# Moving two weight transposes, eight adds, a compare, some bank copies and the row turns inside a decoder kernel

## The reference

```
x = LN(x + attention(x))             # 16 heads of 8, rotary positions, causal
x = LN(x + cross(x, ctx, mask))      # 16 heads of 8, with biases
x = LN(x + experts(x))               # 8 experts of 512, the best 2 per token
x = LN(x + attention(x))             # "wide": 16 heads of 64, not causal
x = LN(x + cross(x, ctx, mask))      # 16 heads of 8
x = LN(x + proj(LN(gelu(fc(x)))))    # weights rounded to -1, 0, 1
```

## Time and profile before

| | |
|---|---|
| three executions | 369.69, 370.45, 370.66 us (median 370.45) |
| profiled execution, its own time | 367.09 us |
| its span | 365.1 us |
| granted TensorE clock, mean | 0.970 |
| TensorE / VectorE / ScalarE / GpSimd busy | 88% / 63% / 50% / 52% |
| stream `pre` and its drain | to about 120 us |
| routed experts | about 120 to 195 us |
| stream `post` | about 200 us to the end |

### The profile page before, as it was taken

How to read it: one execution, slowest core, us unless ns; L and a number is a source line. 1 busy time by engine, 2 the same in 40 slices (tenths; PEclk the granted TensorE clock), 3 DMA queues, 4 the chain that set the end, 5 groups by cost and what they waited for, 6 DMA issues and landing times.

```text
span 365.1 us, 10567 instructions
## 1 busy us (share of the span) xinstructions
PE 321.6 (88%) x4062; PEld 265.6 (73%) x4062; DVE 230.6 (63%) x537; ACT 180.8 (50%) x395; POOL 191.6 (52%) x281
## 2 busy tenths in 40 slices
PE   3878998998798599999996897899999988899993
PEld 2546776877697499999995864676778556787763
DVE  1459986788846434573336477845666466787685
ACT  2247776787547533323314243544354443888641
POOL 2526998575677545543305756312222145487685
PEclk9999999899959999999999699999999999999999
DMA  6799998000011211111101110000000000000001
GB/s 190 230 319 266 292 300 246 4 2 4 15 45 38 73 31 46 50 54 45 32 27 36 45 31 16 0 4 0 2 2 2 3 3 2 2 4 2 4 22 36
DMA packets 35978, 23.02 MB, mean 63 GB/s; under 512 B 4160, under 2 KB 33882, under 8 KB 35802
## 3 DMA queue, kind: packets, MB, share of 16 engines
q1 hardware_dynamic: 34618, 19.64, 18.4%
q0 software_dynamic: 1024, 2.10, 2.0%
q10 hardware_dynamic: 288, 0.62, 0.5%
HBM read 14.60 MB, written 7.73 MB: 61 GB/s over the span
## 4 chain that ended last, share of the span: by engine, by line
PE 64%; DVE 14%; issue 8%; POOL 6%; ACT 4%; DMA 3%; SPq 1%; POOLq 0%; ACTq 0%; DVEq 0%
PE banks L933 7%; PE banks L923 7%; PE banks L1741 6%; PE banks L1710 6%; PE banks L1718 6%; PE banks L461 5%; PE banks L634 5%; PE banks L968 3%; PE banks L607 2%; PE banks L560 2%; PE banks L1125 2%; DVE mx L426 2%; PE banks L1483 2%; PE banks L947 2%; PE banks L586 1%
## 5 line engine op out<-in xcount | busy, mean ns | idle before, releaser
L470 ACT ACTIVATE PT<-banks 128x512 f32<-128x512 f32 x64 | 35.0, 598 | 24.3 <-PE banks L461 23.8
L974 ACT ACTIVATE U<-banks 128x512 f32<-128x512 f32 x40 | 23.9, 597 | 36.7 <-PE banks L933 21.3
L1698 POOL COPY U<-WALL 128x1024 f32 x23 | 23.8, 1040 | 32.2 <-PE banks L1718 29.4
L334 POOL TENSOR_SCALAR ve<-mv 128x1 f32<-128x1 f32 x40 | 9.4, 234 | 56.3 <-DVE mv L329 55.7
L1733 DVE TENSOR_TENSOR PT<-banks,PR 128x512 f32<-128x512 f32 x23 | 15.9, 691 | 34.5 <-PE banks L1718 30.3
L449 ACT ACTIVATE PR<-PR 128x1024 f32<-128x1024 f32 x32 | 33.8, 1057 | 7.0 <-DVE PR L443 7.0
L461 PE MATMUL banks<-cst,PR 128*128 128x128 f32 x256 | 34.8, 280 | 0.5 <-DVE rk L1577 0.4
L923 PE MATMUL banks<-XT,WQKV 128*128 128x128 f32 x256 | 33.2, 292 | 0.4 <-ACT XT L1905 0.4
L923 PEld LDWEIGHTS banks<-XT,WQKV 128*128 128x128 f32 x256 | 31.7, 205 | 1.1 <-ACT XT L1905 0.7
L426 DVE TENSOR_REDUCE mx<-banks 128x16 f32<-128x1024 f32 x24 | 29.3, 1219 | 4.7 <-PE banks L618 3.2
L933 PE MATMUL banks<-WALL,XT 128*64 128x512 f32 x128 | 29.8, 601 | 2.8 <-DVE U L974 2.8
(11 more groups left out here) (192 smaller groups left out, 720.6 us busy)
## 6 DMA issues: line engine op xcount, KB each, us to landing
routed_rows<-zero SPq DMA_DIRECT2D x1, 4544.0 KB, 19.5
WALL<-in_L_ffn_wg_dram SPq DMA_DIRECT2D x8, 256.0 KB, 5.5
WALL<-in_L_ffn_wu_dram SPq DMA_DIRECT2D x8, 256.0 KB, 5.8
WALL<-in_L_ffn_wd_dram SPq DMA_DIRECT2D x8, 256.0 KB, 6.4
U<-in_L_attn_W_qkv_dram SPq DMA_DIRECT2D x1, 1536.0 KB, 6.9
XG<-routed_rows SPq DMA_DIRECT2D x23, 64.0 KB, 1.8
routed_rows<-YS SPq DMA_DIRECT2D x23, 64.0 KB, 1.6
cst<-shape_constants ACTq DMA_DIRECT2D x1, 537.0 KB, 4.4
```

What stands on the lines that cost most here:

```text
L470: act.activation(PT[:, n % 2, 4 * m:4 * m + 4, :].rearrange("p r q -> p (r q)"), PS[:, B_PT + m, :], ACT.Copy).then_inc(self.pt.sem, 1)
L974: return eng.activation(o, s, ACT.Copy) if part == 0 else eng.tensor_copy(o, s)
```

## The change

Weight groups 2 and 3 leave `later` and become `weights`, with one bank, number 4. Group 2 is turned in step 4 and copied by ScalarE, group 3 in step 5 and copied by VectorE; TensorE waits for bank 4 to be read before each, and for the copy behind each. The residual adds of `a0` move from steps 3 to 10 (one each) to steps 1 to 4 (two each). The bias adds that follow `a0` move from steps 6 to 13 to steps 10 to 17. The compare for `mrb` moves from VectorE, step 4, to GpSimd, step 5. ScalarE copies all wide fills below 20. A wide tile's row is turned in front of the q projection instead of behind the transposes of exponentials, its copy stands ahead of ScalarE's q copy, and the waits are changed to match; where the last wide tile meets the first narrow one, the narrow tile's transposes come before the wide tile's weighted values.

```diff
-        later = Transposes("later", [x_group(1), c_group(0), c_group(1), ([], [(gw[:, :], 8)], gwT[:, :]), w_group(1), w_group(2)], [6, 7])
+        later = Transposes("later", [x_group(1), c_group(0), c_group(1), ([], [(gw[:, :], 8)], gwT[:, :])], [6, 7])
+        weights = Transposes("weights", [w_group(1), w_group(2)], [4])
...
             def x_pe(self, pe, job):
                 pe.wait_ge(*self.norm.ln.at(i + 1))
                 if self.wide:
-                    if i + 1 < NT:
-                        pe.wait_ge(*self.norm.r.at(i + 2))
-                    beside = job.ahead(5)
+                    last = job.ahead(4)
+                    if last.stage.narrow:
+                        pe.wait_ge(*last.stage.q_read(last.i))
+                        pe.wait_ge(*last.stage.k_read(last.i))
...
             def x_act(self, act, job):
-                o, k = job.after, job.ahead(5) if self.wide else job.ahead(6)
-                if o and o.stage.narrow and not self.wide:
+                o, b = job.after, job.ahead(5)
+                if self.wide and b.stage.narrow:
+                    act.wait_ge(*(b.stage.k_mm if b.k_first() else b.stage.q_mm).at(b.i + 1))
+                elif o and o.stage.narrow and not self.wide:
                     act.wait_ge(*o.r_read())
...
             def by(self, f):
-                return DVE_FILLS[self.kind(f)]
+                return DVE_FILLS[self.kind(f)] if f >= 20 else 0
...
             # va_pe of wide tiles
                 if job.before:
                     pe.wait_ge(*job.before.r_read())
-                if job.ago(2):
-                    pe.wait_ge(*job.ago(2).x_read())
+                    pe.wait_ge(*job.before.x_read())
...
             # stream_pe
+                for x in turned(tiles, j):
+                    if x.stage.wide:
+                        x.stage.x_pe(pe, x)
                 if b:
                     b.stage.q_pe(pe, b)
...
-                if v and v.stage.wide:
+                last_wide = v and v.stage.wide and t and not t.stage.wide
+                if v and v.stage.wide and not last_wide:
                     v.stage.va_pe(pe, v)
                 if t:
                     t.stage.t_pe(pe, t)
+                if last_wide:
+                    v.stage.va_pe(pe, v)
...
             # stream_act
+                for x in turned(tiles, j):
+                    if x.stage.wide:
+                        x.stage.x_act(act, x)
                 if b:
                     b.stage.q_act(act, b)
...
         def pre_pe(pe, j, part):
             if j in (1, 2) and part == 2:
-                later.pe(pe, ((0, 1), (2, 3, 4, 5))[j - 1])
+                later.pe(pe, ((0, 1), (2, 3))[j - 1])
...
+            if j in (4, 5) and part == 0:
+                for s in pre[j - 3].v_read():
+                    pe.wait_ge(*s)
+                if j == 5:
+                    pe.wait_ge(*pre[0].y_read())
+                weights.pe(pe, (j - 4,))
+            if j in (4, 5) and part == 1:
+                weights.done(pe, j - 3)
...
             # pre_act
+            if j == 4 and part == 1:
+                weights.copies(act, 0, (0,))
...
             # pre_dve
+            if j == 5 and part == 0:
+                weights.copies(dve, 1, (1,))
...
-            if j == 4 and part == 1:
-                dve.tensor_scalar(mrb[0:6, :, :], mri[0:6, :, :], 0.0, None, ALU.is_equal).then_inc(s_mk, 1)
...
         def pre_pool(pool, j, part):
-            pass
+            if j in (1, 2, 3, 4) and part == 2:
+                for i in (2 * j - 2, 2 * j - 1):
+                    a0.res_pool(pool, pre[i])
+            if j == 5 and part == 2:
+                pool.wait_ge(s_m, 16 * 4)
+                pool.tensor_scalar(mrb[0:6, :, :], mri[0:6, :, :], 0.0, None, ALU.is_equal).then_inc(s_mk, 1)
+            if j >= 10 and part == 2 and j - 10 < NT:
+                a0.bias_pool(pool, pre[j - 10])
...
             # sync
+            weights.done(sp)
             later.done(sp)
```

More of the change, by code:

```diff
@@ L355, in decoder_kernel @@
             y_dve = ya_dve = sum_dve = max_dve = sub_dve = qk_dve = none
-            mask_pool = blocks_pool = cos_pool = res_pool = hidden_pool = bias_pool = shares_pool = none
+            mask_pool = blocks_pool = cos_pool = hidden_pool = bias_pool = shares_pool = none
             wide = early = narrow = False
@@ L375, in x_pe @@
                     beside = job.ahead(6)
-                if beside and beside.stage.narrow:
-                    for s in beside.first_read():
-                        pe.wait_ge(*s)
+                    if beside and beside.stage.narrow:
+                        for s in beside.first_read():
+                            pe.wait_ge(*s)
                 if self is a1 and i == 2:
@@ L1309, in stream_pe @@
                     t.stage.t_pe(pe, t)
+                if last_wide:
+                    v.stage.va_pe(pe, v)
                 if v:
                     v.stage.vb_pe(pe, v)
-                for x in turned(tiles, j):
-                    x.stage.x_pe(pe, x)
                 if b and b.stage.narrow and not b.k_first():
                     b.stage.k_pe(pe, b)
+                for x in turned(tiles, j):
+                    if not x.stage.wide:
+                        x.stage.x_pe(pe, x)
                 if y:
@@ L1343, in stream_act @@
                 for x in turned(tiles, j):
-                    x.stage.x_act(act, x)
+                    if not x.stage.wide:
+                        x.stage.x_act(act, x)
                 if b and b.stage.narrow and not b.k_first():
@@ L1407, in stream_pool @@
                 for x in turned(tiles, j):
-                    x.stage.bias_pool(pool, x)
-                if t:
-                    t.stage.res_pool(pool, t)
+                    if tiles is post:
+                        x.stage.bias_pool(pool, x)
                 extra(pool, j, 2)
@@ L1934, in pre_act @@
             if j in (1, 2) and part == 2:
-                later.copies(act, 0, ((0, 1), (2, 3, 4, 5))[j - 1])
+                later.copies(act, 0, ((0, 1), (2, 3))[j - 1])
+            if j == 4 and part == 1:
+                weights.copies(act, 0, (0,))
             if j == len(pre) and part == 1:
@@ L1940, in pre_dve @@
             if j in (1, 2) and part == 2:
-                later.copies(dve, 1, ((0, 1), (2, 3, 4, 5))[j - 1])
+                later.copies(dve, 1, ((0, 1), (2, 3))[j - 1])
+            if j == 5 and part == 0:
+                weights.copies(dve, 1, (1,))
             if j == 3 and part == 1:
```

6 lines of the change are left out of this document (2 added, 4 removed).

## The result

The first measurement gave 357.69 us against 370.07, a ratio of 0.9739 (95% interval 0.9685 to 0.9793). The profiled execution took 356.69 (span 354.9), against 367.09 (365.1). The change was then measured again in two sittings, on two chips.

| | runs | lowest | median | mean | highest |
|---|---|---|---|---|---|
| before, all | 59 | 365.08 | 367.37 | 367.81 | 374.01 |
| changed, all | 16 | 356.53 | 361.24 | 361.05 | 366.79 |
| before, kept | 54 | 365.08 | 367.27 | 367.42 | 370.66 |
| changed, kept | 11 | 356.53 | 359.03 | 359.46 | 363.37 |

What follows compares the result with a forecast made beforehand. TensorE, busy 88% of 365.1 us, was taken as the main bound, with VectorE and GpSimd full from 42 to 47. 2.8 + 2.4 + 0.85, called 6.1, off the median 370.45 gave 364.3, range 361.0 to 367.8.

Steps and rivals of the forecast that it cites:

- The level: Whole kernel: the gain was taken from the three runs' median 370.45, 3.4 above the profiled 367.09, giving 364.3.
- The sum: Whole kernel: 2.8 for the first stream, 2.4 for fills and 0.85 for turned rows, called 6.1 us.
- part 3: Second stream's wide fills on ScalarE: TensorE's stalls of 1.84 and 0.93 go, XT costs 0.69; 2.4 us gained.
- part 4: Second stream, steps 9 to 12: wide rows turned earlier end q projections' waits for XT; 0.85 us gained.
- part 2: First stream: residual adds moved off GpSimd's steps 6 to 8 and compare onto GpSimd; 0.4 us gained, once.
- The range: Whole kernel: 361.0 to 367.8 us at 8 in 10; under 1.1 us counted as no change.
- rival A: TensorE's instruction-stream pause near 63 and slow pace, 2.7 us: gone, 361.6 (chance 0.12); another, 367.0 (0.18, shared with B).
- part 1: First stream: weight groups 2 and 3 leave step 2; 4.1 us less 0.96 and 0.5 leaves 2.65.
- allowance: Step 3 of the first stream: TensorE mostly at fast pace; 0.2 us allowed, 0.9 if all slow.
- B: Steps 4 and 5: weight transposes cost 2.05 each, or a late input uses up 4.1; 367.0, shared chance 0.18.
- C: Step 10: mask rows landing after 61.2 delay tile 8's scores, making the kernel slower; chance 0.04 with its like.
- Theory P: From the held-back-load experiments: TensorE pauses without releaser come from instruction transfers among loads on the same DMA engines.

Runs made afterwards that it cites:

- e5: The changed kernel measured again without edit, beside the kernel before: 360.52 us against 367.39, ratio 0.9830.
- e12: The changed kernel with the narrow stages' x turned ahead of the k projection again: 362.11 us, ratio 0.9857 to the kernel before.
- e11: The changed kernel with residual adds, bias adds and compare back in their old places: 363.39 us, ratio 0.9874 to the kernel before.
- e8: The kernel before with only the wide fills below 20 moved to ScalarE: 364.69 us, ratio 0.9902 to the kernel before.
- e2: The kernel before with wide fills on ScalarE, turned rows and the new places of x and k: 364.75 us, ratio 0.9944 to the kernel before.
- e6: The changed kernel with loads of W_qkv and experts 4 to 7 held back until step 10's scores: 361.85 us, ratio 0.9781 to the kernel before.
- e9: The changed kernel measured a third time, on the chip of the last three experiments: 362.48 us against 367.23, too wide for a ratio.
- e7: The kernel before with loads of W_qkv and experts 4 to 7 held back until step 10's scores: 366.29 us, ratio 0.9979.
- e10: The changed kernel with only wide tile 7's row turned late, behind step 12's k projection: 361.73 us, ratio 0.9834 to the kernel before.

## Why the prediction missed

**The level, the step that failed.** The sum of 6.1 stands between the runs' differences (6.1 to 8.2) at their lower end. But "there is time in them that I cannot see; I take the same difference from the median" carried it from 367.09 to 370.45. That median of three was high: of the 56 other runs of the kernel before only seven reach 369.69, the lowest of those three, and the median of all 59 is 367.37, next to the profiled execution's 367.09. From there the sum gives 361.3, against 361.24 over all runs of the changed kernel and 359.03 over those kept. The first measurement's 357.69 is the same thing on the other side: three of its four runs are among the four fastest of sixteen, and the fourth is the slowest. So of the 6.6 us between forecast and measurement 3.1 are the level and 3.5 lie between 357.69 and the median of all sixteen. By that share, seven of 56, three runs of the kernel before would all lie so high once in some 500 times if each were drawn by itself; what held them together, when the fourth of that sitting took 365.42, is open.

**The sum, right in part by luck.** It left out the swap of x and k, which gave 0.5 to 1.0 from s4 to s10 and 0.13 behind, and put part 3 0.4 too low; part 4 gave 0.5 to 0.6 less than forecast and part 2 0.1 to 0.4 less. Together the stretches give about 6.4: 2.1 up to s4, 1.1 to s10 (28.08 to 26.97, the mean of five), 0.1 to s15, 2.8 for the fills and 0.3 for the rows.

**The range, the second failure.** I knew one pause of 1.20 and one slow stretch, made rival A of them, and gave it 2.7 us and 0.12; and I took 1.1 us for what can't be told from no change, where single runs of the kernel before scatter with a standard deviation of 1.9. The runs show such things in many places. Step 3 ran at full pace in two of the nine executions that had part 1 and cost about 1 us more in the rest; the pauses from s4 to s10 take 0.17 (e5) to 3.29 (e12) together; s15 to W0 moves by 3.3 us. Its first part, up to the first gathered tile, in windows of e5 and e11:

```profile
82.97:116.34 33.37, 24.57 (x290) 21.30 (x286) 24.04 (x109) 20.11 (x47) 22.40 (x29) 0.95 0.11 37
```
```profile
85.00:122.58 37.58, 29.99 (x289) 26.58 (x286) 23.87 (x109) 20.32 (x47) 21.77 (x28) 0.77 0.10 32
```

But for one bias add on GpSimd these are the same instructions, with a granted clock of 0.95 in 33.37 us and of 0.77 in 37.58. The changed kernel's runs span 10 us. A range of 6.8 around one number had no room for them.

**Part 1, right.** Scores of tile 1 at 19.1 forecast, 19.21 to 19.45 in nine executions. In the first profile step 4 lost 1.03 (5.31 for 4.28) where I had 0.96, step 5 0.33 (5.52 for 5.19) where I had 0.5. The 0.80 in step 5, though it names no releaser, stands in all nine executions: it is the wait for VectorE's copy that I had walked, not a pause like the others. Up to s4 the nine average 34.71, against 36.82 for the five without part 1: 2.1, where 2.65 less an allowance of 0.2 was forecast. The term that was mis-sized is the allowance: the slow pace is the usual case there, not the rare one. "The change takes the 2.56 us pause out, so I count on the fast one" is refuted: TensorE was slow before that pause already (in the kernel before, too, four transposes at 17.45 take 1.12), and step 3 is fast only where the first full clock is granted before 19.2 us, at 15.01 and 18.39 in the two fast cases, and at 22.91 to 25.44 in six slow ones. In the ninth, e12, it came at 13.50 and the clock fell again from 20.32 to 23.74. Beyond s4 part 1 gave another 0.2 to 0.4 that was not forecast (the table behind e12).

**Part 2, 0.4 forecast, 0 to 0.3 found.** Alone its ratio is 1.0027 (0.9997 to 1.0057). What shortens steps 7 to 9 is in the main the swap of x and k, which I had put at nothing without a reason, and not the adds that leave GpSimd. GpSimd's compare cost 1.51 and not 1.04, within my bounds, and nobody waited for it.

**Part 3, 2.4 forecast, 2.79 in all nine executions that have it.** Both stalls went, as said. The price for XT was 0.41 rather than 0.69: W0 to the third tile's projections takes 10.43 in e8 and 10.02 before. 1.84 + 0.93 - 0.41 is 2.36, and the short gaps make up the rest. It reached the upper bound.

**Part 4, 0.85 forecast, 0.26 measured against e8 (0.35 against the kernel before).** In the walk, step 9 was right (0.57 forecast, 20.81 to 20.27 is 0.54). Step 10 lost 0.12 of it. After step 11 I had 1.3 and the traces have 0.42 + 0.44 = 0.86 (step 11 takes 5.38 for e8's 5.81); in step 12 I had 0.4 given back, and 0.60 was (5.44 for 4.84). The wait that replaces the one removed is longer: 1.67 for the row, in front of everything, for 1.16 in front of q. In two of seven executions with this wait the clock then fell, for 1.6 us; in none of the six without part 4 did it. So part 4 may well be worth nothing, which the ratios of e2 (0.9944) and e8 (0.9902) can't exclude.

**Rivals.** A came and went between executions of the same program (0.44, 0.17 and 1.26 in the changed one), so it was no property of the change; in the first profile most of it had gone, by luck. B did not happen: see part 1's terms. C did not happen: the scores of tile 8 waited for no mask rows.

**What stays open.** Theory P rests on the pauses moving with the loads and on the transfers of 16,384 bytes that precede each; why such a transfer starts later in one execution than in another is open, and no run took the transfers away. The Trainium skill, "Runtime: NRT & Kernel Launch", section "Instruction fetch mechanics", has instructions arriving in blocks of 16 KiB (256 instructions) and calls the crossing of a block mostly hidden. The traces agree with both, the size and the hiding, from 48 to 61 in e6, with the loads away, and do not agree with the hiding for the 0.44 to 1.26 at one and the same instruction among the loads. Why a clock falls behind a stall in one execution and not in the next is open, and no kernel here beats the changed one by more than its spread.

## What to carry to other kernels

Before a forecast is tied to a median, compare it with the profiled execution and ask how many runs stand behind it; the single runs of the changed program scatter with a standard deviation of 3.3 us here, those of the one before with 1.9, and the difference of the first two medians, 12.4, was twice the 6.1 of all runs. Go through the diff line by line before the sum: the swap of two short pieces of TensorE's queue, left out here, was worth more than the eight adds that were priced. Size an edit in the stretch where it acts: the fills' 2.79 was exact in every trace, while the totals gave 2.1 to 3.6. When a row is brought forward in an engine's queue, look for the one that is not ready yet; the other seven gained, and the last made TensorE stand 1.67 us with its whole queue behind it.

## What the runs showed of the hardware

- A pause of TensorE with no releaser stays at one instruction and varies in length: 0.44 (changed) and 1.26 (e9) before the fourth of eight mask matmuls. With the loads taken away (e6, e7) none over 0.12 stood from s9 to s10. The 31 such pauses from step 6 to step 14 all end 2.2 to 2.7 us after the start of a 16,384-byte instruction transfer.
- A pause hides under a stall: the 0.96 of e10 appeared where the other executions stand 1.67 for a row.
- Whether half pace follows a stall varies: after the same wait in step 12 the granted clock stayed at 1.00 (changed) or fell to 0.50 (e5).
- TensorE starts each of the fourteen executions at the slow pace, and full clock is first recorded at 13.50 to 26.42 us. The windows print 1.00 ahead of that first entry (sixteen scores took 1.16 in e5 beside such a 1.00, and 0.69 later), so the pace there is to be read from the matmuls.
- A compare of 6x512 int32 elements took 1.51 on GpSimd and 0.73 on VectorE.
